# Reordering one software-pipelined schedule: the fourth quad of self-attention estimates, a norm, and a value projection move

## The reference

```
h  = layernorm(x)
x1 = x + tanh(g_x) * (softmax(split(h Wq + bq) @ split(ctx Wk + bk)^T / sqrt(8)) @ split(ctx Wv + bv) @ Wo + bo)   # 16 heads of 8
h2 = rms(layernorm(x1)) ; q, k = rms per head(h2 wq^T), rms per head(h2 wk^T) ; v = h2 wv^T
a  = softmax(causal(q k^T / sqrt(8))) v wo^T      # columns 0..31 set to 0
x2 = layernorm(x1) + a
xf = rms(x2) ; gates = top-2 of 4 of softmax(xf gate^T), renormalised
moe = sum of gates * 4 expert MLPs(xf)            # columns 0..31 set to 0; all experts are run
out = x1 + tanh(g_f) * (x2 + moe)
```

## Time and profile before

| | |
|---|---|
| median of 3 runs | 1189.64 us (1189.31 to 1192.32) |
| the profiled execution, its own time | 1192.36 us |
| its span, first to last instruction | 1190.6 us |
| PE (TensorE matmul) busy | 1038.0 us, 87% |
| DVE (VectorE) busy | 792.6 us, 67% |
| ACT (ScalarE) busy | 735.7 us, 62% |
| POOL (GpSimd) busy | 351.5 us, 30% |
| DMA, share of 16 engines | 37.2% |
| TensorE clock granted, mean | 0.94 of full speed |

### The profile page before, as it was taken

The page is one execution under the profiler, slowest core; times in us unless marked ns, Lnnn a source line. Parts: engine busy times, 40 slices in busy tenths (PEclk is TensorE's granted clock), DMA queues, the critical chain, the costliest instruction groups (busy, mean ns, idle before and its releaser), DMA issues.

```text
span 1190.6 us, 26283 instructions
## 1 busy us (share of the span) xinstructions
PE 1038.0 (87%) x8578; PEld 645.1 (54%) x8578; DVE 792.6 (67%) x2153; ACT 735.7 (62%) x1329; POOL 351.5 (30%) x522
## 2 busy tenths in 40 slices
PE   3647798999999998999999999999999898988797
PEld 1324455555555565555565665555565555555454
DVE  7266666767777767777767676767767676764523
ACT  1334566767576666767666766767666676756353
POOL 4611415133141414133141514224141513214030
PEclk8667789999999999999999999999999999999899
DMA  5144444433434444333344444334344443220300
GB/s 179 32 119 107 120 108 120 110 101 90 103 67 115 119 116 119 90 99 99 93 88 115 119 116 106 90 100 98 79 114 115 119 114 98 82 45 34 83 1 18
DMA packets 78693, 114.27 MB, mean 96 GB/s; under 512 B 9153, under 2 KB 41537, under 8 KB 78529
## 3 DMA queue, kind: packets, MB, share of 16 engines
q1 hardware_dynamic: 78368, 111.58, 37.2%
q10 hardware_dynamic: 288, 2.21, 0.5%
HBM read 58.97 MB, written 53.74 MB: 95 GB/s over the span
## 4 chain that ended last, share of the span: by engine, by line
PE 55%; issue 17%; DVE 15%; ACT 6%; POOL 3%; DMA 2%; SPq 2%; DVEq 0%; POOLq 0%; ACTq 0%
PE ps_w L1157 11%; PE ps_pv L1131 7%; PE ps_s2a L1110 7%; PE ps_s2b L1110 5%; DVE mpadB L888 4%; PE ps_w L1175 4%; PE ps_t L1016 3%; PE ps_w L1016 3%; PE ps_w L1060 3%; DMA qdB<-mTB 2%; SPq L528 2%; PE ps_w L1092 2%; ACT probs L766 2%; DVE mpadA L888 2%; PE ps_w L1030 2%
## 5 line engine op out<-in xcount | busy, mean ns | idle before, releaser
L766 ACT ACTIVATE probs<-ps_s2a 120x512 f32<-120x512 f32 (+1 forms) x256 | 152.9, 597 | 129.7 <-PE ps_s2a L1110 124.6
L888 DVE TENSOR_REDUCE mpadA<-ps_w 128x4 f32<-128x480 f32 x256 | 150.3, 652 | 50.6 <-PE ps_w L1092 50.6
L888 DVE TENSOR_REDUCE mpadB<-ps_w 128x4 f32<-128x512 f32 x256 | 158.8, 685 | 28.9 <-PE ps_w L1092 28.9
L1157 PE MATMUL ps_w<-W,hid 128*128 128x96 f32 x1024 | 142.4, 298 | 18.6 <-DVE split_q L797 16.0
L1157 PEld LDWEIGHTS ps_w<-W,hid 128*128 128x128 f32 x1024 | 134.9, 212 | 33.8 <-DVE split_q L797 20.8
L766 ACT ACTIVATE probs<-ps_s2b 120x512 f32<-120x512 f32 (+1 forms) x256 | 152.6, 596 | 0.2 <-PE ps_s2b L1110 0.2
L666 POOL TENSOR_SCALAR_AFFINE_SELECT probs<-probs 128x1024 f32<-128x1024 f32 x128 | 140.0, 1093 | 0.0
L630 POOL TENSOR_TENSOR rB<-veB,neg_half 128x4 f32<-128x4 f32 x16 | 16.1, 1008 | 394.4 <-DVE veB L790 394.4
L1110 PE MATMUL ps_s2a<-qdB,kstB 128*128 128x512 f32 x128 | 66.1, 517 | 38.9 <-DMA qdB<-mTB 32.5
L1175 PE MATMUL ps_w<-xfT,W 128*128 128x512 f32 x160 | 85.0, 620 | 0.0
L665 POOL TENSOR_TENSOR tick<-one 128x1 f32<-128x1 f32 x128 | 24.9, 195 | 186.9 <-ACT probs L766 183.1
(11 more groups left out here) (176 smaller groups left out, 2096.3 us busy)
## 6 DMA issues: line engine op xcount, KB each, us to landing
scratch_Aq<-split_q SPq DMA_DIRECT2D x48, 256.0 KB, 2.4
qdA<-scratch_Aq SPq DMA_DIRECT2D x64, 192.0 KB
scratch_Bq<-split_q SPq DMA_DIRECT2D x48, 256.0 KB, 2.4
scratch_Bk<-split_k SPq DMA_DIRECT2D x48, 256.0 KB, 3.0
qdB<-scratch_Bq SPq DMA_DIRECT2D x64, 192.0 KB
kstB<-scratch_Bk SPq DMA_DIRECT2D x64, 192.0 KB
scratch_Ak<-split_k SPq DMA_DIRECT2D x48, 240.0 KB, 2.9
kstA<-scratch_Ak SPq DMA_DIRECT2D x64, 180.0 KB
```

Of the source, the lines that this page charges most:

```text
L766: nc.scalar.activation(probs[0:k, slot_of(part, *index), :], bank[0:k, :], ACT.Exp, scale=SCALE if part == "A" else 1.0).then_inc(done, 1)
L888: nc.vector.tensor_reduce(mneg[OP[part]][:, :, c, b], bank[:, 0:HT * k].rearrange("p (h k) -> p h k", h=HT), AX.X, ALU.max, negate=True).t ...
L1157: ins = mm(bank[:, b * UP:(b + 1) * UP], hid[:, HID_AT[h] + k, b * P:(b + 1) * P], w[f"down{index[1]}"][:, k * UP:(k + 1) * UP], start=k = ...
```

## The change

It is made of edits to the lists of uses, and one to DVE's order in the ramp.

- In `first_experts` the fourth quad of B estimates is taken out; it now ends `cross_attention`, behind the third quad of A's values and ahead of the logits. `B mT` moves from behind `N v` to behind `A nT 1`; `gates 0` moves behind `A oT 1`, `A norm` behind `N v`.
- In `second_experts` `N norm` moves from behind D's squares to ahead of `D wo 1` (the residual), and `D squares` behind `B qT` and `B kT`.
- `B v` moves from ahead of the first pair of A's exact scores to behind it.
- The step t = 1 (`third_group`) makes B's four quads one place earlier each, with `N xT` later and `B mT` ahead of `N q`.
- The step t = 16 (parts B, D, M), which took the common list, has its own, `last_self_keys`, in which B's queries, keys and estimates come earlier.
- Where a step lacks a part, DVE makes A's block-diagonal keys ahead of the low part of the key split instead of behind it.

```diff
 def second_experts():
...
             + one("N", "stats", 0, None)
-            + one("D", "nT", 1, "t") + one("A", "mT") + fill("M", "e2_l3", 0) + one("D", "wo", 1, "t")
-            + one("D", "out", 0, None) + one("D", "squares", 0, None) + one("N", "norm", 0, None) + one("B", "qT") + one("B", "kT")
+            + one("D", "nT", 1, "t") + one("A", "mT") + fill("M", "e2_l3", 0) + one("N", "norm", 0, None) + one("D", "wo", 1, "t")
+            + one("D", "out", 0, None) + one("B", "qT") + one("B", "kT") + one("D", "squares", 0, None)
             + fill("M", "e2_l3", 1, "w"))
 def cross_attention():
-    return (one("B", "v") + exact("A", 0, 0) + down(2) + exact("A", 0, 2) + one("N", "xT")
+    return (exact("A", 0, 0) + one("B", "v") + down(2) + exact("A", 0, 2) + one("N", "xT")
...
-            + values("A", 2) + one("D", "logits") + one("A", "nT", 0, "t"))
+            + values("A", 2) + estimate("B", 3) + one("D", "logits") + one("A", "nT", 0, "t"))
 def first_experts():
     return (fill("D", "e1_w1", 0, "w") + one("A", "wo", 0, "t") + fill("D", "e1_w2", 0, "w") + values("A", 3)
-            + one("D", "gates", 0, None) + fill("D", "e1_w1", 1, "w") + one("A", "oT", 1, "t") + fill("D", "e1_w2", 1, "w")
-            + one("A", "nT", 1, "t") + fill("D", "e2_l1", 0) + one("A", "wo", 1, "t") + one("A", "stats", 0, None)
-            + one("N", "base", 0, None) + estimate("B", 3) + fill("D", "e2_l1", 1) + fill("D", "e3_down", 0) + one("N", "q")
-            + one("D", "gates", 1, None) + one("A", "norm", 0, None) + one("N", "v") + one("B", "mT") + one("N", "k")
+            + fill("D", "e1_w1", 1, "w") + one("A", "oT", 1, "t") + one("D", "gates", 0, None) + fill("D", "e1_w2", 1, "w")
+            + one("A", "nT", 1, "t") + one("B", "mT") + fill("D", "e2_l1", 0) + one("A", "wo", 1, "t") + one("A", "stats", 0, None)
+            + one("N", "base", 0, None) + fill("D", "e2_l1", 1) + fill("D", "e3_down", 0) + one("N", "q")
+            + one("D", "gates", 1, None) + one("N", "v") + one("A", "norm", 0, None) + one("N", "k")
             + fill("D", "e0_up", 0) + one("D", "gates", 2, None) + fill("D", "e0_up", 1, "w") + one("D", "gates", 3, None))
 def third_group():
...
-            + exact("A", 2, 0) + one("N", "xT") + exact("A", 2, 2) + values("A", 1)
-            + exact("A", 3, 0) + one("A", "oT", 0, "t") + estimate("B", 1) + exact("A", 3, 2) + values("A", 2)
-            + one("A", "nT", 0, "t") + one("A", "wo", 0, "t") + values("A", 3) + estimate("B", 2)
+            + exact("A", 2, 0) + estimate("B", 1) + exact("A", 2, 2) + one("N", "xT") + values("A", 1)
+            + exact("A", 3, 0) + one("A", "oT", 0, "t") + estimate("B", 2) + exact("A", 3, 2) + values("A", 2)
+            + one("A", "nT", 0, "t") + one("A", "wo", 0, "t") + values("A", 3) + estimate("B", 3)
             + one("A", "oT", 1, "t") + one("A", "nT", 1, "t") + one("A", "wo", 1, "t")
-            + one("A", "stats", 0, None) + one("N", "base", 0, None) + estimate("B", 3)
-            + one("N", "q") + one("A", "norm", 0, None) + one("N", "v") + one("B", "mT") + one("N", "k"))
+            + one("A", "stats", 0, None) + one("N", "base", 0, None) + one("B", "mT")
+            + one("N", "q") + one("N", "v") + one("A", "norm", 0, None) + one("N", "k"))
+def last_self_keys():
+    return (of_parts("BDM", self_attention())
+            + fill("M", "e2_l2", 0) + one("D", "wo", 0, "t") + one("B", "scale", 0, None) + fill("M", "e2_l2", 1)
+            + values("D", 3) + fill("M", "e3_up", 0) + one("D", "oT", 1, "t") + one("B", "qT") + one("B", "kT")
+            + fill("M", "e3_up", 1) + one("D", "nT", 1, "t") + fill("M", "e2_l3", 0) + one("D", "wo", 1, "t")
+            + one("D", "out", 0, None) + one("D", "squares", 0, None) + estimate("B", 0) + fill("M", "e2_l3", 1, "w")
+            + one("B", "v") + down(2) + estimate("B", 1)
+            + one("D", "norm", 0, None) + one("B", "init", 0, None) + one("B", "copy", 0, None)
+            + down(3) + one("M", "store", 0, None) + estimate("B", 2) + one("D", "xfT") + one("D", "logits")
+            + fill("D", "e1_w1", 0, "w") + fill("D", "e1_w2", 0, "w") + estimate("B", 3)
+            + fill("D", "e1_w1", 1, "w") + one("D", "gates", 0, None) + fill("D", "e1_w2", 1, "w")
+            + fill("D", "e2_l1", 0) + one("B", "mT") + fill("D", "e2_l1", 1) + fill("D", "e3_down", 0)
+            + one("D", "gates", 1, None) + fill("D", "e0_up", 0) + one("D", "gates", 2, None)
+            + fill("D", "e0_up", 1, "w") + one("D", "gates", 3, None))
...
-TAIL = [(NG - 1, "ABDM", of_parts("ABDM")), (NG, "BDM", of_parts("BDM")), ...
+TAIL = [(NG - 1, "ABDM", of_parts("ABDM")), (NG, "BDM", last_self_keys()), ...
...
                     elif (part, work) in (("N", "q"), ("N", "k")):
+                        if work == "k" and st.parts != PARTS:
+                            block_diagonal_keys(part, "A", g)
                         low_part(st, "N", "A", work, ALU.add, col["b" + work])
                         if work == "k":
-                            block_diagonal_keys(part, "A", g)
+                            if st.parts == PARTS:
+                                block_diagonal_keys(part, "A", g)
```

More of the change, by code:

```diff
@@ L160, with of_parts @@
 SCHEDULE = self_attention() + second_experts() + cross_attention() + first_experts()
+def of_parts(parts, order=None):
+    return [use for use in order or SCHEDULE if use[0] in parts]
 def first_group():
@@ L245, in uses_before @@
     return n
-def of_parts(parts):
-    return [use for use in SCHEDULE if use[0] in parts]
 PARTS = "NABDM"
@@ L255 @@
 LOOP = (3, NG - 1)
-TAIL = [(NG - 1, "ABDM", of_parts("ABDM")), (NG, "BDM", of_parts("BDM")), (NG + 1, "DM", last_self_values()), (NG + 2, "M", last_experts())]
+TAIL = [(NG - 1, "ABDM", of_parts("ABDM")), (NG, "BDM", last_self_keys()), (NG + 1, "DM", last_self_values()), (NG + 2, "M", last_experts())]
 assert all(sorted(map(str, order)) == sorted(map(str, of_parts(parts))) for _, parts, order in RAMP + TAIL)
```

## The result

The changed kernel takes 1213.31 us, the median of four runs (1212.46 to 1214.1), against 1189.47 us for the kernel before on the same chip (1189.07 to 1192.32). The ratio is 1.0195 with a 95% interval of 1.0177 to 1.0213. It is slower; the prediction said 1164.0, 1144 to 1183. The profiled execution has a span of 1212.3 us against 1190.6 and a mean granted clock of TensorE of 0.93 against 0.94.

A forecast was written before the change was run, and what follows sets the result against it. TensorE's work plus its in-order queue's waits was taken as the bound. Terms -15.4, 0, +12.4, -12.5, -6.2 and -4 gave -25.7 from the profiled 1192.36 us: 1166.7 profiled, 1164.0 median, range 1144 to 1183.

The forecast's parts named there:

- Entry: Start of cross-attention: norm earlier, squares and `B v` later remove the 1.29 us wait before `down(2)`; -1.1 us a step.
- End of the step: Quad and `mT` earlier: 2.47 us of waits gone, 2.45 new before quad, logits, `e3_down` and first pair; net 0.
- e3_down: Expert matmul late in the step: its bank waits for a GELU behind a table load and `mT`'s copy; 0.4 us.
- Opening: Start of the next step: chain from `N q` 2.1 us late, delaying `hT` 0.45 and fourth `B qk` 0.5; +0.95 a step.
- Clock: TensorE's clock: eleven old falls to the lower level go (-16.5 us), three new ones come (4); -12.5 in all.
- The rival that I gave 0.16: TensorE's clock keeps falling once a step behind the new waits at quad and logits; 1176.5 us, chance 0.16.
- The rival of a second fall: The clock falls at both the logits and the next step's start in all 14 steps; 1197.5 us, chance 0.08.
- Ramp: Steps before the loop: keys' order -2.4 us, later bank of `hT` +0.8, waits gone in t = 1 -4.6; together -6.2.
- The keys' order: Steps t = 0 and 1: block-diagonal keys ahead of the low part save 1.2 us each, -2.4 together.
- t = 16: Step behind the loop with its own list: one new wait of about 2.5 us against two old ones; -2.5.
- Table-switch rival: The GELU before `e3_down` comes later by another table load, 1.28 us in 13 steps; 1181 us, chance 0.04.
- t = 15: First step behind the loop, without part N: loses one clock fall, -1.5 us.

The follow-up runs named there:

- One swap: The changed kernel with POOL's `xb` (N base) put ahead of A's statistics: 1191.29 us, ratio 1.0 to the kernel before.
- the entry's body in two kernels: The kernel before with only the cross-attention reordering (`N norm`, `D squares`, `B v`): 1165.81 us; the same plus the new t = 1 list and keys' order: 1161.28 us.

## Why the prediction was wrong

The forecast was -25.7 and the span grew by 21.7, a miss of 47. By its own steps:

- **Entry, -1.1 a step: right**, measured -1.35 (the 0.2 left for ScalarE was not needed, and no loop step waits for the pair's own maxima).
- **End of the step, 0: right**, in each piece that the trace shows: no DMA wait, no wait before `down(2)`, 1.05 and 0.85 where 1.1 and 0.85 were written, 0.37 for `e3_down` where 0.4 was. What is left for this term of the measured step, 67.05 - 66.35 + 1.35 - 2.37 (the next point) = -0.3, agrees.
- **Opening, +0.95 a step (bounds 0 and 1.9): wrong in size, and past its bound.** From the start of the first pair to that of the third it takes 606.05 - 598.76 = 7.29 in the changed kernel and 642.21 - 637.29 = 4.92 at full clock without the quad's move: +2.37. The step of the reasoning that failed is "is done near 662.0" for the keys' low part: I shifted DVE's chain by 2.1 as a block and kept its durations. But `A norm` (hb) and the gates shifted against POOL as well, and a two-input operation of the gates ahead of `hb` came to lie beside `xb`: 0.8 us. One swap gave it back (0.85 a step at full clock). Without it the same stretch takes 6.41, so the opening costs 1.5, within the bounds. A trace of it was in the profile before, a 0.39 where its like took 0.18. I had not asked why.
- **Clock, -12.5: wrong, and the largest miss.** "I take three falls of 14 for the new one": the twelve loop steps had 15, against ten before, 1.6 us each. In the loop the forecast had some -11 and the runs show about +9 (with the rounding of the windows), a miss of 20. Its reason, that two waits of 1.95 us with 0.6 of small matmuls between are milder than one of 2.22, does not hold: in eleven loop steps of twelve a fall followed the two, and where the quad stood behind the logits and they were gone, so were the falls. The rival that I gave 0.16 was right in this, though it too had one fall a step. The trace agrees with what the Trainium skill (TensorE: Matmul & The Clock Gate, A second HAM failure mode: psum-queue depth-cycling) says of short idles at PSUM banks; here they are waits of 1.05 and 0.85 us. The rival of a second fall, 0.08, had a fall at the logits and another in the opening. No loop step has both; what three of them have is a fall of double length, 6.8 us, at the logits. Why double is open.
- **Ramp, -6.2: right alone** (1191.57 - 1186.25 = 5.3), by other parts: -8.8 before the first pair of D where -7.0 was forecast, and t = 2 +4.4, not about -1. The keys' order was sized too high: at A's first exact pair of t = 1 (89.77 before, 89.14 now) 0.6 of its 2.4 had come; the list of t = 1 brought 8.2 where 4.6 was forecast. Of t = 2's +4.4, 2.6 is busy time of TensorE at a clock of 0.85 for 0.88 (51.72 to 54.28), and TensorE newly waits there for `hb`, which did not come sooner with the rest:

```profile
120.49 1.11 PE L1036 MATMUL ps_w<-identf,hb 128*128 128x128 f32 x4 [3.32 <-DVE hb L851]
```

- **t = 16, -2.5: wrong sign.** +8.9, of which 6.3 is TensorE's busy time (49.40 to 55.70) at a clock of 0.83 for 0.92. I counted one new wait against two old ones. Of the two old ones the 2.64 went and the 2.38 for the DMA fell to 1.7; what came is one of 3.12 and, at the step's start, one of 1.78 for `hb`. Waits of about a microsecond stand in both kernels. All idle time together grew by 2.6 us, the rest of the 8.9:

```profile
1113.25 3.75 PE L1188 MATMUL ps_w<-hid,W 128*128 128x512 f32 x4 [3.12 <-DVE mpadB L908]
1122.11 0.40 PE L1108 MATMUL ps_w<-causal_k,causal_q 32*128 32x512 bf16 x4 [1.25 <-DVE ym L937]
```

- **Table-switch rival:** not borne out; `e3_down`'s 0.37 leaves no room for the 1.28 more of that rival.

By stage the loop alone makes some 31 of the 47 us (17 from the opening, 20 from the clock, less 6 from entry and end), t = 16 another 11.4, ramp and t = 15 the rest.

In short, nearly every wait at the step's end was named beforehand. What was missed is that durations on DVE depend on what POOL does beside it, and that whether the clock falls did not follow from how much idle time there is: 1.9 us in two pieces had a fall behind it in nearly every loop step. With `xb` first the change is even with the kernel before (1191.29), with the quad behind the logits it is a gain (1170.18), and with both and the common list in t = 16 it takes 1153.19, below the 1164.0 forecast.

What stays open: that the same body with the same waits has falls in some steps and none in others is shown (the entry's body in two kernels, the quad's move alone within one execution), but not what decides it; and the waits before the quad and before the logits were only taken away together, in an edit that moved `wo 0` too.

## What to carry to other kernels

When a chain is moved on one engine, lay the moved instructions beside the other engine's timeline again: here short two-input operations of DVE that started under a GpSimd operation of 1.1 to 1.3 us were stretched to its end, and one swap of independent work freed the one that TensorE waited for. Price a reorder at full clock first (a step whose granted clock is 1.00 in both kernels), then the clock apart, and count two waits of a microsecond close together like one of two: here both kinds of hole were followed by a fall in most steps, and by none in some. A removed wait pays only if nothing of its size takes its place; here, once the clock was up, a step without the DMA wait of 2.2 us (65.05) was no shorter than one with it (65.0), since other waits had come.

## What was not expected of the hardware

- DVE operations of 16 elements with two inputs in SBUF took 0.91 to 0.98 us in place of 0.18 to 0.23 where they started under GpSimd's `xb` or mask, ending within 0.04 us of it, in three places of two kernels. Beside GpSimd's `tick`, 0.19 us long, their like kept 0.17. GpSimd's own durations did not change (`xb` 1.26 us in the changed kernel, 1.28 before; the mask 1.09).
- The same loop body had a fall in two steps of three in one kernel and in none of nine consecutive steps in another, which differ only in the ramp; and the quad's move alone went within one execution from six steps without a fall (68.4) to five with one of double length (71.6), the body being the same.
